# The first network's row of attention targets by way of memory, and two more pieces of the second product ahead of the attention turns

## What is computed

```python
# first network: 3 layers, one head, for each graph
si, sj = x @ attn_w[l, :d], x @ attn_w[l, d:]            # a source and a target score per node
scores = leaky(si[:, :, None] + sj[:, None, :] + attn_b[l])
attn = softmax(where(mask, scores, -inf))                # mask: adj + identity
h = layernorm(x + attn @ x)
x = layernorm(h + gelu(h @ W1[l] + b1[l]) @ W2[l] + b2[l])
# after the 3 layers: x = layernorm(x0 + x)
# second network: one layer, 8 heads, on the same adj without the identity
xp = x @ W_proj
scores = leaky(a_src[..., None] + a_dst[..., None, :] + b_att)
out = layernorm(x + relu(softmax(masked scores) @ xp))
```

## Time and profile before

| | us |
|---|---|
| median of 3 runs | 2467.51 |
| lowest, highest | 2463.15, 2467.58 |
| the profiled execution | 2463.12 |
| its span in the trace | 2461.3 |
| TensorE busy | 2316.7 (94%) |
| ScalarE busy | 1775.4 (72%) |
| VectorE busy | 1673.3 (68%) |
| DMA queue of SP, share of the 16 engines | 16.3% |

### The profile page before, as it was taken

How to read it: one execution, slowest core, us unless ns; L and a number is a source line. 1 busy time by engine, 2 the same in 40 slices (tenths; PEclk the granted TensorE clock), 3 DMA queues, 4 the chain that set the end, 5 groups by cost and what they waited for, 6 DMA issues and landing times.

```text
span 2461.3 us, 33928 instructions
## 1 busy us (share of the span) xinstructions
PE 2316.7 (94%) x11329; PEld 1644.5 (67%) x11329; DVE 1673.3 (68%) x5652; ACT 1775.4 (72%) x3406; POOL 170.9 (7%) x199
## 2 busy tenths in 40 slices
PE   2999999999999999999999999999999999999765
PEld 1676666767766766776677677667666766776543
DVE  6445865587656866678665877468775686666487
ACT  1434477877878768887787878787687876888676
POOL 0000100000000100000000001000000000000000
PEclk9999999999999999999999999999999999999876
DMA  5111211012111121012120121110320111200110
GB/s 182 35 35 35 68 58 60 24 60 86 44 52 48 39 96 60 22 57 76 46 69 22 65 84 35 63 48 31 103 60 18 52 61 35 69 19 17 31 44 30
DMA packets 85768, 131.57 MB, mean 53 GB/s; under 512 B 4408, under 2 KB 53852, under 8 KB 85596
## 3 DMA queue, kind: packets, MB, share of 16 engines
q1 hardware_dynamic: 85596, 129.41, 16.3%
HBM read 120.74 MB, written 8.65 MB: 53 GB/s over the span
## 4 chain that ended last, share of the span: by engine, by line
PE 78%; ACT 11%; DVE 7%; issue 3%; DMA 0%; POOL 0%; SPq 0%; DVEq 0%; POOLq 0%; ACTq 0%
PE ffn L1047 21%; PE ffn L1034 12%; PE av L1034 12%; PE av L991 12%; PE pT L975 11%; PE av L1006 4%; ACT prob L439 3%; PE av L1073 3%; DVE prob L677 2%; ACT prob L433 2%; PE av L1021 2%; ACT xs L467 1%; PE trow L956 1%; ACT prob L426 1%; PE ffn L1045 1%
## 5 line engine op out<-in xcount | busy, mean ns | idle before, releaser
L1047 PE MATMUL ffn<-w_sb,G 128*128 128x256 f32 x3072 | 745.6, 380 | 0.0
L1047 PEld LDWEIGHTS ffn<-w_sb,G 128*128 128x128 f32 x3072 | 551.2, 191 | 73.9 <-issue 13.2
L677 DVE CUSTOM_DVE_ANT_0 prob<-trow,mask 128x512 f32<-128x512 f32 x704 | 458.0, 686 | 177.2 <-PE trow L956 147.5
L975 PEld LDWEIGHTS pT<-ident,prob 128*128 128x128 f32 x2816 | 355.5, 145 | 200.9 <-issue 125.7
L975 PE MATMUL pT<-ident,prob 128*128 128x128 f32 x2816 | 440.8, 282 | 39.0 <-DVE prob L722 21.4
L439 ACT ACTIVATE prob<-prob,nm 128x512 f32<-128x512 f32 x512 | 362.6, 711 | 0.0
L1034 PE MATMUL ffn<-hT,w_sb 128*128 128x512 f32 x768 | 357.4, 595 | 1.1 <-ACT hT L452 1.1
L1034 PE MATMUL av<-hT,w_sb 128*128 128x512 f32 x768 | 355.7, 593 | 0.0
L433 ACT ACTIVATE prob<-prob,s 128x512 f32<-128x512 f32 x512 | 347.3, 713 | 9.8 <-DVE nm L684 9.8
L448 ACT COPY prob<-pT 128x512 f32<-128x512 f32 x444 | 254.5, 579 | 94.1 <-PE pT L975 93.3
L393 POOL TENSOR_TENSOR rstd<-veps,mhalf 128x4 f32<-128x4 f32 x128 | 153.6, 1200 | 2279.9 <-DVE veps L612 2279.9
(11 more groups left out here) (97 smaller groups left out, 2502.8 us busy)
## 6 DMA issues: line engine op xcount, KB each, us to landing
w_sb<-in_L_gnn_W SPq DMA_DIRECT2D x48, 1024.0 KB, 7.5
trow<-rows_dram SPq DMA_DIRECT2D x128, 256.0 KB, 3.2
adj_sb<-in_adj SPq DMA_DIRECT2D x16, 1024.0 KB, 5.4
xin<-in_x SPq DMA_DIRECT2D x16, 512.0 KB, 6.4
x0r<-in_x SPq DMA_DIRECT2D x16, 512.0 KB, 4.5
out<-o SPq DMA_DIRECT2D x16, 512.0 KB, 3.3
aw_row<-in_L_gnn_attn_w SPq DMA_DIRECT2D x1, 768.0 KB
g_row<-in_L_gnn_g SPq DMA_DIRECT2D x2, 384.0 KB
```

What stands on the lines that cost most here:

```text
L677: return v.tensor_tensor_reduce(out=out_[:, t, :], in0=targets, in1=mask[:, t, :], scale=1.0, scalar=LEAST, op0=ALU.add, op1=ALU.max, accu ...
L975: last = te.transpose(pT[bank][:, j * P:(j + 1) * P], src[:, t, j * P:(j + 1) * P], ident[:])
L1047: last = te.matmul(ffn[part][:, at:at + D], G[:, f, t * P:(t + 1) * P], w2_sb[:, g // 2 % STAGES, f, :], start=False, stop=f == FT - 1)
```

## The change

The first network's target row no longer passes TensorE. SP waits for the scores, stores the 512 targets of a unit to a buffer in memory (one element of 4 bytes at a time, since the column lies across partitions), waits until that has landed, and loads them back broadcast to 128 partitions, into an SBUF tile `trow0` that replaces the PSUM bank. In SP's order this stands behind the weights and ahead of the head rows. On TensorE `first_target_row` is gone, pieces 4 and 5 move ahead of the attention (six pieces are ahead of it), pieces 6 and 7 take their places inside the attention, and the first two transposed tiles of the second head have no piece behind them. ACT's and DVE's orders stay as they are.

```diff
@@
         trow1 = sb("trow1", [P, ROWS, N])
+        trow0 = sb("trow0", [P, N])
@@
-        trow0 = pb("trow", [P, N])
@@
+        s_rowst0 = sem("rowst0")
@@
+        rows0_dram = nc.dram_tensor("rows0_dram", (UNITS, N), F32, kind="Internal").ap()
@@
+            def first_row(u):
+                sp.wait_ge(s_st, u + 1)
+                sp.dma_start(rows0_dram[u].rearrange("(t p) -> p t", p=P), raw0[:, 1, :],
+                             allow_slow_non_contiguous=True).then_inc(s_rowst0, 16)
+                sp.wait_ge(s_rowst0, 16 * (u + 1))
+                if u:
+                    sp.wait_ge(s_mt, u)
+                sp.dma_start(trow0[:], rows0_dram[u].partition_broadcast(P)).then_inc(s_trow, 16)
+
+            first_row(0)
@@
                 if g % 2 == 0 and g and g + 2 < UNITS:
                     sp.wait_ge(s_ff2, PARTS * g)
                     load_weights(g // 2 + 1)
+                if g + 1 < UNITS:
+                    first_row(g + 1)
                 if begun(g) is not None and begun(g) % 2 == 0:
@@
             def first_targets(s):
-                dve.wait_ge(s_trow, c("trow"))
+                dve.wait_ge(s_trow, c("trow", 16))
@@
-            c.skip("mt", -1)
@@
-            def spread(row, col):
-                for t in range(T):
-                    last = te.transpose(row[:, t * P:(t + 1) * P], col[:, t:t + 1].broadcast_to([P, P]), ident[:])
-                return last
-
-            def first_target_row():
-                pe.wait_ge(s_st, c("st"))
-                if c.due("mt"):
-                    pe.wait_ge(s_mt, c.now("mt"))
-                spread(trow0, raw0[:, 1, :]).then_inc(s_trow, 1)
@@
-            first_target_row()
             attention(0, 0, 0, lambda i: None)
@@
-                    if f == FT - 2 and att:
-                        first_target_row()
                     first_product(g, f)
@@
-                for t in range(T):
-                    piece(t)
+                for n in range(T + 2 * att):
+                    piece(n)
                 if att:
-                    attention(s2, l2, g + 1, lambda i: piece(4 + i))
+                    attention(s2, l2, g + 1, lambda i: piece(6 + i))
                 else:
                     last_graph_begins()
@@
                 for t in range(T):
                     for q in heads[1:2]:
                         turn(q, t)
-                    if att or t >= DT:
+                    if t >= DT:
                         piece(6 + t)
```

## The result

The changed kernel takes **2954.52 us** (median of 4 runs, 2945.35 to 2957.11) against 2466.98 (4 runs, 2463.15 to 2467.58): **1.1978 times** the time, interval 1.1963 to 1.1993. That is 487 us more; 87 had been forecast, and the range ended at 2616.

What follows compares the result with a forecast made beforehand. TensorE, busy 94% of the span, was taken as the bound. Terms -20.4 + 4.2 + 56.7 + 47 = +87.5 us over the profiled 2463.1 gave 2550.6, stated as 2552 for the median; range 2498 to 2616.

Steps and rivals of the forecast that it cites:

- step 2: Row by way of memory: store 2.2 us, load 3.2, wake-ups 0.1, so x = 5.5; uncovered at the start, +4.2 us.
- upper end: Bound on the store's landing time: 3.3 us, from the output's 512 pieces of 1 KB.
- slow store: Rival: the store of 4-byte pieces takes 5 us instead of 2.2, x is 8.3, total 2643 us; chance 0.09.
- x: Time from the end of the scores to DVE's first tile of targets; 2.73 us before, 5.5 forecast, bounds 4.8 and 6.6.
- Step 1: TensorE's four transposes go, 0.434 us in each of 47 units: -20.4 us.
- a saving there is worth its full length: TensorE hardly waits between 480 and 2270 us, so time saved on its instructions shortens the unit by as much.
- Step 3: TensorE's piece 3 waits for GELU 7, x - 4.03 us in 27 units, more in units 1 to 5: +56.7 us.
- No wait: Units of k = 0 and k = 2: scores end some 7.4 us ahead of the row, so 5.5 us causes none.
- Step 4: Two pieces moved ahead of the attention no longer cover TensorE's waits for ACT's copies and the state: +47 us.
- The order costs nothing: Rival: ACT's lead at the copies is larger than read, total 2504 us; chance 0.12 jointly with the row being in time.
- faster: Rival: the transposes' saving stays whole and neither piece 3 nor the copies are late, total 2446 us; chance 0.03.

Runs made afterwards that it cites:

- E6: Changed kernel without the store and its wait, row loaded from the network's input, old order of the pieces: 2465.24 us, ratio 0.9993.
- E5: Changed kernel without the store and its wait, row loaded from the network's input, new order of the pieces kept: 2517.99 us, ratio 1.0200.
- E4: Changed kernel with its 512 pieces of 4 bytes stored 512 bytes apart and the row loaded from the network's input: 2551.66 us (one run).
- E3: Changed kernel with the row stored as 128 pieces of 16 bytes side by side, targets permuted: 2581.42 us, ratio 1.0468.
- F1: Changed kernel with its 512 pieces of 4 bytes stored 16 bytes apart and the row loaded from the network's input: 2609.87 us (one run).
- E1: Kernel before with only the new order of the pieces, the row still made by TensorE: 2525.59 us, ratio 1.0242.
- G2: E3 with the old order of the pieces: 2554.54 us, ratio 1.0363.
- G3: F2 with the old order of the pieces: 2536.95 us (one run).
- F2: Changed kernel with its 512 pieces of 4 bytes stored 64 bytes apart and the row loaded from the network's input: 2554.1 us (one run).
- E8: Changed kernel with GELU 7 and the copy behind it ahead of the next attention's four scores on ACT: 2797.0 us, ratio 1.1354.
- E2: Changed kernel with the old order of the pieces, the row still by way of memory: 2958.36 us, ratio 1.1997.
- G1: Changed kernel storing 128 pieces of 16 bytes, DVE reading the row with a 16-byte step, old order of the pieces: 2630.11 us, ratio 1.0649.

## Why the prediction was right or wrong

**The direction and the mechanism held; the time was outside the range by 338 us, and the step that failed is step 2, "I take 2.2 us: nearer the small store".** The store took 8.4. What made it fail is the "upper end" beside it: the output's 512 pieces of 1 KB bounded the number of pieces, not what was new about this store, that its pieces lie side by side, sixteen of them to 64 bytes. No row of before had such writes, so 3.3 was no bound. The rival of the slow store had the right sign of that doubt, but was priced at 5 us, again from the same row. A further 1.2 us of x is the load: behind this store it landed in 4.4 us, where the prediction took the head rows' 3.2. Of the 402 us above the forecast 285 are the longer wait for GELU 7, 7 the start, and 102 the slower work that the prediction had no term for; the median stands the rest above the profiled execution.

**Step 1** (transposes, -20.4): they are gone from TensorE's list, but the saving is not collected. E6 has no transposes, the old order and x = 3.4 us, below the prediction's limit of 4.03, and is still at 0.9993: the start costs 2.9 us more, units 1 to 4 1.1 to 1.4 each and unit 5 3.3, and in later units the gain is 0.8 in k = 0, 0.4 in k = 2 and about nothing elsewhere. In those units TensorE gives the time back at the attention, whose inputs now come later: in unit 9 the 0.44 us of the transposes are gone, a wait of 0.20 stands at L991, and the transposed tiles and products around it take 0.26 more from start to start, at a clock of 1.00. So the prediction's "a saving there is worth its full length" did not hold where the other engines' lead was short. The row by memory reaches DVE 0.7 us later than through TensorE (x of 3.4 against 2.7), even with no store at all.

**Step 3** (piece 3 behind GELU 7) held, mechanism and slope. The formula, with the measured x in place of 5.5 (x - 2.3 in units 1 to 4, x - 1.4 in unit 5):

| | x | x - 4.03 in 27 units | units 1 to 5 | k = 0, k = 2, others | formula | measured |
|---|---|---|---|---|---|---|
| E5 | 3.4 | 0 | 6.4 | 0 | 6 | 5.9 |
| E4 | 5.2 | 31.6 | 15.4 | 0 | 47 | 41.0 |
| E3 | 5.6 | 42.4 | 17.4 | 0 | 60 | 56.8 |
| F1 | 5.9 | 50.5 | 18.9 | 0 | 69 | 65.8 |
| changed kernel | 13.2 | 247.6 | 55.4 | 43 (measured) | 346 | 341.7 |

"No wait" for k = 0 and 2 was said of x = 5.5, with 7.4 us of cover. At 13.2 these units wait too, and so do units 0 and 6, 43.2 us together; the formula has no term for them, and the column takes what was measured. The 27 units waited 243.8 us and units 1 to 5 54.8. E4, whose pieces have 64 bytes and more to themselves, has the time that was forecast for the change, 2552, though its x was 0.3 us smaller than taken and its profiled execution stands 17 us above what transposes, start and waits add up to (9 of them work at the low clock): the agreement is partly luck.

**Step 4** (+47) held for the waits, 47.4 measured in the changed kernel and in E1 alike: copies in 41 places, the state in 8. In time the order costs 58, since work at the low clock comes on top. Its last sentence, that ahead of the attention the pieces "cover nothing that was bare", holds only for a row in time. With the later row they cover the exponentials, and the order costs 17 to 27 us in place of 53 (G2, G3 against E3, F2).

**A missing term: slower work behind a wait.** The prediction summed waits as if the work behind them kept its length. By the estimates above some 93 of the 482 us, and 11 of E1's 61, are work at the low clock; the little that is left is of the size of the lost overlap. It is not shown how the clock depends on a wait's length; the low level followed 8.9 us of idle in unit 21, and 2.1 us in some units of E1 but not in others.

**The rivals.** "The order costs nothing" is out (E1), "faster" too (E6: even a row from one load alone is not clear of the kernel before). "Slow store" was the case that came, at a chance of 0.09, with its price too low.

**Left open.** What in the memory makes neighbouring small writes slow; the size of the block that counts (above 16 bytes, since F1 is slower than F2, and no more than 64, since F2 and E4 are alike; "the same 64 bytes" is this text's reading); why 16-byte pieces at the same distance land sooner than 4-byte ones (1.4 against 2.5), where the number of pieces differs too; whether it matters that neighbouring pieces may be written by different ones of the 16 DMA engines, which the trace does not name; and why the same store took 8.2 us in E8, 8.4 in the changed kernel and 9.0 in E2.

## What to carry to other kernels

Before a small result is sent through memory to turn it from a column into a row, write down how many separate writes fall within 64 bytes of each other; with sixteen of 4 bytes the landing here was 8.4 us, with four 2.5, with one 1.8, and with four of 16 bytes 1.4. A bound must come from a row that shares that feature, not only the count. Where all engines run in lockstep on in-order queues, price a late value by who stands behind its waiter on the next engine (here a GELU tile behind two scores), and add to each wait of TensorE what the work behind it loses at a lower clock. A slower path is worth having only in the units that have the cover for it: here 8 of 48, for 0.2% of the time.

## What the runs showed of the hardware that was not expected

- Stores of 4-byte pieces from 128 partitions: landing 8.4 us (512 pieces) and 7.0 (128) side by side, 2.5 at 16 bytes' distance, 1.8 at 64 and at 512; 128 pieces of 16 bytes side by side 1.4.
- A broadcast load of 2 KB to 128 partitions landed in 3.8 us (E3) and 4.4 us (changed kernel) when it read what a store of small pieces had just written, in 3.1 when it read `x` (E4), and in 3.1 (E3) when it read head rows that had just been written.
- TensorE's granted clock was 0.50 behind an idle time of 8.9 us and 0.53 behind one of 2.12 us in unit 13 of E1, but 1.00 behind one of 2.12 us in its unit 19.
- A new wait costs TensorE more than the idle time shown: 0.50 us for 0.33 in unit 10 of E1, at a clock of 1.00.
- DVE's fused add and maximum over 128x512 in float32 takes 684 ns on a row as it lies and 1077 ns when the row is read with a step of 16 bytes (G1; the mask and the output are not strided).
